# Attention block on one core: the causal mask of the diagonal score blocks moves from TensorE to ScalarE and GpSimd, and PSUM banks are handed over two at a time

## The reference

```
h = _layernorm(x, axis=-1) * (1 + ca) + sa
# inside the attention: q, k rotated, 16 heads of 8 channels
scores = jnp.einsum('bhqd,bhkd->bhqk', q, k) * scale
scores = jnp.where(causal_mask, -jnp.inf, scores)
attn = jax.nn.softmax(scores, axis=-1)
out = jnp.einsum('bhqk,bhkd->bhqd', attn, v)
...
x = x + ga * _L0_attn_ref(h, ...)
h = _layernorm(x, axis=-1) * (1 + cb) + sb
x = x + gb * _L0_ffn_ref(h, ...)
```

## Time and profile before

| | |
|---|---|
| median of 3 runs | 369.53 us (368.46 to 371.78) |
| span of the profiled execution, first to last instruction | 368.0 us (the page gives no other time of it) |
| busy in the span | PE 340.0, DVE 258.0, ACT 208.2, POOL 103.8 us |
| mean granted PE clock | 0.986 |

### The profile page before, as it was taken

The page is one execution under the profiler, slowest core; times in us unless marked ns, Lnnn a source line. Parts: engine busy times, 40 slices in busy tenths (PEclk is TensorE's granted clock), DMA queues, the critical chain, the costliest instruction groups (busy, mean ns, idle before and its releaser), DMA issues.

```text
span 368.0 us, 6868 instructions
## 1 busy us (share of the span) xinstructions
PE 340.0 (92%) x2332; PEld 160.5 (44%) x2360; DVE 258.0 (70%) x563; ACT 208.2 (57%) x399; POOL 103.8 (28%) x189
## 2 busy tenths in 40 slices
PE   6999789999799898999999989999999999899886
PEld 4545345443354432443543434344434445434555
DVE  4947667987999977587667878677887777423254
ACT  5350056754166666677356665864666665785341
POOL 3543253427410424401301212101204232443221
PEclk9999889999999999999899999999999999999999
DMA  6547512221410003340230500500000000000000
GB/s 202 184 118 189 139 44 69 67 67 25 113 44 0 3 1 73 74 101 0 67 89 6 130 2 2 131 1 30 1 2 3 3 3 1 4 0 3 28 2 29
DMA packets 13314, 18.87 MB, mean 51 GB/s; under 512 B 4192, under 2 KB 9184, under 8 KB 13280
## 3 DMA queue, kind: packets, MB, share of 16 engines
q1 hardware_dynamic: 12992, 18.04, 18.4%
q10 hardware_dynamic: 288, 0.39, 0.3%
HBM read 12.98 MB, written 5.24 MB: 50 GB/s over the span
## 4 chain that ended last, share of the span: by engine, by line
PE 67%; issue 9%; DVE 8%; POOL 3%; ACT 2%; DMA 0%; SPq 0%; ACTq 0%; POOLq 0%; DVEq 0%
PE ps_o L1066 18%; PE ps L1029 15%; PE ps L1046 13%; PE ps L1000 4%; PE ps L987 4%; DVE tmax L864 3%; PE ps L936 3%; PE ps L1024 2%; DVE rot L760 1%; PE ps L1008 1%; PE ps L993 1%; PE ps L927 1%; PE ps L940 1%; ACT pt L660 1%; PE ps L947 1%
## 5 line engine op out<-in xcount | busy, mean ns | idle before, releaser
L864 DVE TENSOR_REDUCE tmax<-ps 128x1 f32<-128x512 f32 (+3 forms) x304 | 186.4, 656 | 65.4 <-PE ps L1029 65.0
L660 ACT ACTIVATE pt<-ps 128x512 f32<-128x512 f32 (+1 forms) x304 | 161.9, 576 | 105.6 <-PE ps L1046 104.1
L1029 PE MATMUL ps<-kst,qst 72*128 72x128 bf16 (+3 forms) x576 | 113.9, 274 | 3.6 <-issue 2.2
L1046 PE MATMUL ps<-qst,kst 75*128 75x512 bf16 (+3 forms) x384 | 111.0, 327 | 4.9 <-DVE rot L760 1.8
L1066 PE MATMUL ps_o<-pt,v_sb 128*32 128x512 f32 (+3 forms) x768 | 83.5, 507 | 2.0 <-ACT pt L660 1.1
L1029 PEld LDWEIGHTS ps<-kst,qst 72*128 72x128 bf16 x576 | 49.1, 98 | 70.0 <-ACT pt L660 17.9
L556 POOL TENSOR_SCALAR_AFFINE_SELECT pt<-pt 128x512 f32<-128x512 f32 x64 | 40.4, 641 | 68.0 <-ACT pt L660 67.5
L1046 PEld LDWEIGHTS ps<-qst,kst 75*128 75x128 bf16 x384 | 34.9, 98 | 29.6 <-issue 6.4
L1008 PE MATMUL ps<-maska,identb 128*128 128x512 bf16 x118 | 34.1, 396 | 3.5 <-POOL maska L483 3.3
L521 POOL CAST negp<-negm 128x16 bf16<-128x16 f32 x16 | 3.2, 198 | 94.4 <-DVE negm L781 94.2
L1066 PEld LDWEIGHTS ps_o<-pt,v_sb 128*32 128x32 f32 x768 | 15.5, 108 | 32.2 <-issue 17.3
(11 more groups left out here) (102 smaller groups left out, 250.8 us busy)
## 6 DMA issues: line engine op xcount, KB each, us to landing
qst<-qparts SPq DMA_DIRECT2D x48, 96.0 KB
kst<-kparts SPq DMA_DIRECT2D x48, 96.0 KB
qparts<-part SPq DMA_DIRECT2D x16, 96.0 KB, 1.9
kparts<-part SPq DMA_DIRECT2D x16, 96.0 KB, 1.9
xs<-in_x SPq DMA_DIRECT2D x4, 256.0 KB, 7.2
rope_sb<-in_rope SPq DMA_DIRECT2D x2, 512.0 KB, 6.2
qparts<-part SPq DMA_DIRECT2D x16, 64.0 KB, 1.8
qst<-negt SPq DMA_DIRECT2D x48, 4.0 KB, 1.7
```

The costliest lines, as they stand in the source:

```text
L660: act.activation(pt[:, G % NP, h0:h0 + nh, 0:w], src, ACT.Exp, scale=SCALE).then_inc(s_exp, 1)
L864: dve.tensor_reduce(dst, src, AX.X, ALU.max).then_inc(s_max, 1)
L1029: last = pe.matmul(dst[:, j * nk:(j + 1) * nk], qst[0:ROWS, half, h, r * P:r * P + P], kst[0:ROWS, kh, h, k0:k0 + nk], start=(kind != "dia ...
L1046: last = pe.matmul(dst[:, j * w:(j + 1) * w], kst[:, kh, h, kt * P:kt * P + P], qst[:, half, h, c0:HALF], start=True, stop=True)
```

## The change

Three things change. First, the product with `maska` is gone from pass A. A diagonal pair of banks is copied by ACT from PSUM into a buffer `dg` in SBUF (`copy_diagonal`), masked there by POOL (`mask_diagonal`), and reduced by DVE from SBUF `DIAG_LAG` = 6 slots later. `dg` has two halves of 128x1024 and lies over buffers of the first stage (`pro`), so the first copy also waits for the gates. Second, banks go in units of two, in both passes: PE signals after the second bank of a unit, and DVE or ACT reads both with one instruction if they are neighbours in the ring (where the ring ends between them, with two). The two diagonal units of a step come first in its pass A. A unit is written in its first slot; the numbers of slots stay as they were. Third, PE takes pass B before pass A in a slot.

```
-def bank_jobs_a(half):
+def bank_units_a(half):
+    units = [("diag", [(r, 0), (r + 1, 0)], HG, P) for r in range(0, TU, 2)]
     for r in range(TU):
-        jobs.append(("diag", r, 0, HG, P))
         if r:
             nh = min(HG, HALF // (r * P)) if r < 3 else 1
-            jobs += [("tri", r, h, nh, r * P) for h in range(0, HG, nh)]
+            banks = [(r, h) for h in range(0, HG, nh)]
+            units += [("tri", banks[j:j + 2], nh, r * P) for j in range(0, len(banks), 2)]
         if half:
-            jobs += [("sq", r, h, 1, HALF) for h in range(HG)]
-    return jobs
+            units += [("sq", [(r, h), (r, h + 1)], 1, HALF) for h in range(0, HG, 2)]
+    return units
...
+UNIT_B = 2
+NB = 7
+DIAG_LAG = 6
...
-            for bank in grp[3]:
-                b_at[slot] = (s, gi, grp, bank, bank is grp[3][-1])
-                slot += 1
+            for j in range(0, len(grp[3]), UNIT_B):
+                unit = grp[3][j:j + UNIT_B]
+                b_at[slot] = (s, gi, grp, unit, unit[-1] is grp[3][-1])
+                slot += len(unit)
...
+    def operations(kind, i, n):
+        at = [use_no[(kind, (i, j))] % NB for j in range(n)]
+        return [(0, n)] if at == list(range(at[0], at[0] + n)) else [(j, 1) for j in range(n)]
...
+            def mask_diagonal(i):
+                n = diag_no[i]
+                pool.wait_ge(s_dcopy, diag_copies[i][-1])
+                d = dg[:, n % 2]
+                pool.affine_select(out=d, in_=d, compare_op=ALU.is_ge, fill=LOW, base=0,
+                                   pattern=[[0, 2 * HG], [-1, P]], channel_multiplier=1).then_inc(s_dmask, 1)
...
                 if i in b_at and b_at[i][4]:
                     zero_future(*b_at[i][0:3])
+                if i in diag_no:
+                    mask_diagonal(i)
...
+            def copy_diagonal(i):
+                n = diag_no[i]
+                act.wait_ge(s_a, unit_a[i] + 1)
+                if n == 0:
+                    act.wait_ge(s_gated, 1)
+                if n >= 2:
+                    act.wait_ge(s_dmax, n - 1)
+                for j, m in operations("a", i, 2):
+                    b0 = use_no[("a", (i, j))] % NB
+                    act.activation(dg[:, n % 2, HG * j:HG * (j + m)], ps[:, b0:b0 + m, :].rearrange("p b (h k) -> p (b h) k", k=P),
+                                   ACT.Copy).then_inc(s_dcopy, 1)
...
+                if i - DIAG_LAG in diag_no:
+                    s, (_, banks, _, _) = a_at[i - DIAG_LAG]
+                    n, r = diag_no[i - DIAG_LAG], banks[0][0]
+                    dve.wait_ge(s_dmask, n + 1)
+                    dve.tensor_reduce(tmax[STEPS[s][1]][:, s % 2, 0, r:r + 2],
+                                      dg[:, n % 2].rearrange("p (r h) k -> p r h k", h=HG), AX.X, ALU.max).then_inc(s_dmax, 1)
...
-                dst = take("a", i)
-                if kind == "diag":
-                    pe.matmul(dst, identb[:, :], maska[:, :, :].rearrange("p h k -> p (h k)"), start=True, stop=False,
-                              skip_group_check=True)
...
+                for n, (r, h0) in enumerate(banks):
+                    dst = take("a", (i, n))
...
-                if i in a_at:
-                    pass_a(i)
                 if i in b_at:
                     pass_b(i)
+                if i in a_at:
+                    pass_a(i)
```

More of the change, by code:

```diff
@@ L122, in plan @@
     for s, (b, half, g) in enumerate(STEPS):
-        for job in bank_jobs_a(half):
-            a_at[n] = (s, job)
-            n += 1
+        for unit in bank_units_a(half):
+            a_at[n] = (s, unit)
+            n += len(unit[1])
         a_end.append(n)
@@ L202, in adaln_block @@
         group_no.setdefault(b_at[i][0:2], len(group_no))
-    bank_no = {i: n for n, i in enumerate(sorted(b_at))}
+    unit_a = {i: n for n, i in enumerate(sorted(a_at))}
+    unit_b = {i: n for n, i in enumerate(sorted(b_at))}
+    b_slots = {i + j for i in b_at for j in range(len(b_at[i][3]))}
     prep_no = {u: n for n, u in enumerate(PREPS)}
@@ L209, in adaln_block @@
     for i in range(slots):
-        uses += [("a", i)] if i in a_at else []
-        uses += [("b", i)] if i in b_at else []
+        uses += [("b", (i, j)) for j in range(len(b_at[i][3]))] if i in b_at else []
+        uses += [("a", (i, j)) for j in range(len(a_at[i][1][1]))] if i in a_at else []
         uses += [("side", (st[0], st[1], k)) for st in pe_at.get(i, []) for k in range(BANKS_OF.get(st[0], 0))]
     use_no = {use: n for n, use in enumerate(uses)}
+    def operations(kind, i, n):
+        at = [use_no[(kind, (i, j))] % NB for j in range(n)]
+        return [(0, n)] if at == list(range(at[0], at[0] + n)) else [(j, 1) for j in range(n)]
+    diag_no = {i: n for n, i in enumerate(i for i in sorted(a_at) if a_at[i][1][0] == "diag")}
+    max_ops, exp_ops, n_max, n_exp = {}, {}, {}, {}
+    for kind, at, ops, after in (("a", a_at, max_ops, n_max), ("b", b_at, exp_ops, n_exp)):
+        total = 0
+        for i in sorted(at):
+            if i in diag_no and kind == "a":
+                continue
+            ops[i] = operations(kind, i, len(at[i][1][1] if kind == "a" else at[i][3]))
+            for j, n in ops[i]:
+                total += 1
+                for k in range(j, j + n):
+                    after[(i, k)] = total
+    diag_copies, total = {}, 0
+    for i in sorted(diag_no):
+        diag_copies[i] = []
+        for j, n in operations("a", i, 2):
+            total += 1
+            diag_copies[i] += [total] * n
+    max_end = {a_at[i][0]: n_max[(i, len(a_at[i][1][1]) - 1)] for i in sorted(a_at) if i not in diag_no}
+    exp_end = {b_at[i][0:2]: n_exp[(i, len(b_at[i][3]) - 1)] for i in sorted(b_at)}
     qparts = nc.dram_tensor("qparts", (B * 2, NG, 5, HD, HG, HALF), BF16)
@@ L666, in _ @@
                     exp(i)
+                if i in diag_no:
+                    copy_diagonal(i)
                 for st in stages.get(i, []):
@@ L1026, in pass_a @@
-                for j in range(nh):
-                    h = HG * g + h0 + j
-                    k0, kh = (r * P, half) if kind == "diag" else (0, half) if kind == "tri" else (0, 0)
-                    last = pe.matmul(dst[:, j * nk:(j + 1) * nk], qst[0:ROWS, half, h, r * P:r * P + P],
-                                     kst[0:ROWS, kh, h, k0:k0 + nk], start=(kind != "diag"), stop=True,
-                                     skip_group_check=True)
+                for n, (r, h0) in enumerate(banks):
+                    dst = take("a", (i, n))
+                    for j in range(nh):
+                        h = HG * g + h0 + j
+                        k0, kh = (r * P, half) if kind == "diag" else (0, half) if kind == "tri" else (0, 0)
+                        last = pe.matmul(dst[:, j * nk:(j + 1) * nk], qst[0:ROWS, half, h, r * P:r * P + P],
+                                         kst[0:ROWS, kh, h, k0:k0 + nk], start=True, stop=True)
@@ L1042, in pass_b @@
                     pe.wait_ge(s_mstack[s % 2], 48 * (s // 2 + 1))
-                dst = take("b", i)
-                for j in range(nh):
-                    h = HG * g + h0 + j
-                    last = pe.matmul(dst[:, j * w:(j + 1) * w], kst[:, kh, h, kt * P:kt * P + P],
-                                     qst[:, half, h, c0:HALF], start=True, stop=True)
+                for n, (h0, nh) in enumerate(unit):
+                    dst = take("b", (i, n))
+                    for j in range(nh):
+                        h = HG * g + h0 + j
+                        last = pe.matmul(dst[:, j * w:(j + 1) * w], kst[:, kh, h, kt * P:kt * P + P],
+                                         qst[:, half, h, c0:HALF], start=True, stop=True)
@@ L1078, in _ @@
             for i in range(slots):
+                if i in b_at:
+                    pass_b(i)
                 if i in a_at:
                     pass_a(i)
-                if i in b_at:
-                    pass_b(i)
-                if i not in b_at and i < max(a_at):
+                if i not in b_slots and i < a_end[-1] - 1:
                     keep_warm(1)
```

75 lines of the change are left out of this document (44 added, 31 removed).

## The result

The changed kernel takes 402.18 us (median of 4 runs, 398.98 to 405.01) against 370.65 for the kernel before, ratio 1.084 [1.079, 1.089]. The prediction was 379 us, range 363 to 392. Runs of one kernel differ in granted clock and so in time, by up to 4.7%; ratios leave out those over 1.5% above the kernel's fastest, medians do not, and the profiled executions of e1, e2, e4, e6, e7, e13 and e15 are such long ones.

A forecast was written before the change was run, and what follows sets the result against it. PE was taken to bound the kernel (340.0 of 368.0 us busy), with DVE close. Terms -7.0 - 3 + 4.8 + 5.2 + 7.6 + 2 = +9.6 on 368.0 gave 377.6, as a median 379 us; range 363 to 392.

The forecast's parts named there:

- The new waits are under 1 us each, and I count no lower clock for them: PE's added waits across the kernel: each under 1 us, with nothing added for a lower clock.
- the nothing (end: 3.5 us) for (0, 0): Four steps of (0, 0): removing 16 mask products counted as no gain, with 3.5 us as the other end.
- The margin in the ring: PSUM bank ring: paired reads free banks late, PE waits 0.32 us per clean pattern; +4.8 us together, bounds 2.4 to 7.5.
- 16 times with a side step ... which give the reader time: Ring patterns with side steps or narrower banks: 0 to 0.32 us of waiting each, taken as 0.15, 2.4 us together.
- POOL's order: Eight steps with `zero_future` ahead of POOL's four maxima operations: PE waits 0.65 us each, +5.2 us, bounds 0 and 8.
- The diagonal's place: Around the diagonal slots DVE idles, then runs late; PE waits 1.45 us at most of seven places, +7.6 us, bounds 0 and 11.
- the mask: Pass A on PE: dropping 32 mask products in half 1 saves 7.0 us; all 64 at most 14.1 us.
- ACT's copies at nothing: ACT's 32 diagonal copies, at most 1.20 us each, counted as hidden in idle time; up to 13 us if not.
- The short steps: Four steps of (1, 0): DVE needs 9.4 us against 8.72; 0.5 us more each, +2 us, bounds -3.5 and +5.
- The reads in pairs: DVE and ACT reading two banks at once: DVE pair 1.21 us, exponential pair 1.09; -3 us, other end -15.
- The forecast's sign and its reason: Whole kernel: slower, chance 0.60, as the margin, POOL's order and the diagonal's place cost more than the mask did.

The follow-up runs named there:

- e1: Kernel before without the mask product of the diagonal banks, maxima running over future keys too; ratio 0.990 to the kernel before.
- e2: Changed kernel with the mask product back on PE and diagonal banks read by DVE from PSUM, units of two kept; ratio 1.081 to the kernel before.
- e4: Changed kernel with three products without a reader in each of the first 46 slots; ratio 1.089 to the kernel before.
- e6: Changed kernel with the mask product on PE, pass A in units of one bank, pass B in units of two; ratio 1.031 to the kernel before.
- e7: Changed kernel with the mask product on PE, pass A in units of two banks, pass B in units of one; median 397.92 us, no ratio.
- e13: From the fifth step on, diagonal path alone, other units one bank; first four as before except pass B ahead of pass A everywhere; ratio 1.030 to the kernel before.
- e15: Change in the first four steps alone, later steps as before except pass B ahead of pass A in a slot; 388.56 us, ratio 1.048 to the kernel before.
- e5: Changed kernel with two products without a reader in each of slots 11 to 33; 394.38 us, ratio 1.066 to the kernel before.
- e17: Change in the first four steps alone, pass B first everywhere, one product without a reader in each of slots 11 to 33; 380.54 us, ratio 1.027 to the kernel before.
- e14: From the fifth step on, units of two with mask product on PE; first four as before except pass B ahead of pass A everywhere; ratio 1.056 to the kernel before.
- e8: Changed kernel with the mask product on PE and units of one bank in both passes, leaving only the new order; 376.74 us, ratio 1.017 to the kernel before.
- e18: Change in the first four steps alone, pass B first everywhere, two products without a reader in each of slots 11 to 33; 383.86 us, ratio 1.037 to the kernel before.
- e10: Changed kernel with POOL's zeroing of the future weights queued at the unit's last slot again; ratio 1.100 to the kernel before.
- e11: Change from the fifth step on; first four steps as before except pass B ahead of pass A in a slot; 389.31 us, ratio 1.055 to the kernel before.
- e3: Changed kernel with units of one bank in both passes, except diagonal pairs, still copied by ACT and masked by POOL; ratio 1.047 to the kernel before.
- e12: Kernel before without the 19 products without a reader of the first steps; ratio 1.003 to the kernel before.

## Why the prediction was wrong, step by step

**The step that failed first** is "The new waits are under 1 us each, and I count no lower clock for them", with the nothing (end: 3.5 us) for (0, 0). The waits for DVE are about as long as I said (6.0 us in 13, 1.1 at most), but stage B already had a window at 0.84, and what was priced was each wait, not what PE's clock does after several of them. The sum had nothing for B, +7.6 (-7.0 - 3 + 4.8 + 5.2 + 7.6) nearly all in C, and +2 for D. Measured: +14.7, +13.5 and +4.0. In B, some 12 us are the clock: B falls by 12.5 when fillers hold it up in the whole change (e5), and by about as much in the change of the first four steps (e17). The Trainium skill, TensorE: Matmul & The Clock Gate, A second HAM failure mode: psum-queue depth-cycling, tells of a kernel whose PE idles briefly between groups as it cycles through PSUM banks, and whose clock goes to and fro; the falls at 47.6 and 57.8, after 2.14 us of 3.50 and 1.74 of 3.40 with PE busy, agree; the 41 us at half speed that followed are no to and fro.

**The margin in the ring** was right as a mechanism and in its clean place (3.24 us, forecast about 3.2). In the sum, the waits for DVE's maxima were not the large ones: in C they come to 3.7 us in nine places, of each of which the overlap of PE's rows hides up to 0.16, where ring and diagonal had 12.4 (4.8 + 7.6). Yet the units of two, with the order, cost 15.7 us in C (e14), of which 10.2 us at half speed, against 3.4 before, explain at most 3.4. What I had backwards are the "16 times with a side step ... which give the reader time": there the pair delays DVE's work for the side step, and PE's waits for such work in C grow from 2.0 to 6.3 us (3.8 with the order alone, e8). **The order in a slot**, pass B ahead of pass A, had no term of its own: 3 to 5 us in C (e8 +4.6, e18 +5.0; up to 1.7 of each is clock).

**POOL's order**, +5.2, is refuted: 0 (e10). In C, PE waits 1.8 us in four places for POOL's chain, and waited 1.9 in three before.

**The diagonal's place and the mask.** DVE's pattern came as drawn. On top of the units, the diagonal path with the mask product gone gives C 12.1 - 15.7 = -3.6 us (e11, e14; up to 1.7 of it is 3.4 us less at half speed), where my terms made +0.6 (7.6 - 7.0). Without the units it gives C +4.0 (e3), where the order alone gives +4.6 (e8). So in C the path costs about nothing, and what e13 shows is mostly order and clock. With the order counted once (5.0, e18), and half of the half speed that e13 (20.5 us in C) and e14 (10.2) have over e11 (6.8) taken off, 9.0 + 15.7 - 5.0 - 6.8 - 1.7 = 11.2, an estimate, against 12.1 in e11. The mask product alone, at -7.0 for half 1, gave -2.9 in C, seven of its eight steps (e1, with 3.4 us at half speed there as before). **ACT's copies at nothing**: their cover is thin. PE waits 5.6 us in five places for the maxima's rows, but e14, without copies, waits 5.9 in six, so it is not the copies alone that make these rows late.

**The short steps**: +2 forecast (bounds -3.5 and 5), +4.0 measured, +3.4 without the 2.9 us at half speed (e5); e13 gives 3.5 and e14 1.8 of it.

**The reads in pairs** had the right prices: 1.21 us forecast for a pair and for a masked read, 1.219 and 1.208 measured; an exponential of a pair 1.09, measured 1.024. Groups by form after:

```profile
L710 ACT ACTIVATE pt<-ps 128x1024 f32<-128x1024 f32 x99 | 101.0, 1024 | 93.6 <-PE ps L1123 93.4
L940 DVE TENSOR_REDUCE tmax<-ps 128x2 f32<-128x1024 f32 x55 | 66.6, 1219 | 33.6 <-PE ps L1106 33.4
...
L927 DVE TENSOR_REDUCE tmax<-pro 128x8 f32<-128x1024 f32 x32 | 38.7, 1208 | 0.0
```

DVE got 8.9 us back (258.0 to 249.1) and the steps got longer, so the -3 found no place. The forecast's sign and its reason, readers that finish later in a ring of seven, held; the delay of side work, the order in a slot and the late rows of the maxima had no term, and the clock lay outside all bounds. **Open** remain the clock's exact share (the fillers cost time too), which part lets it fall (in B it is at half speed for 10.2 us in e8, 13.7 in e3, 27.3 in e1, 34.1 in e2 and 47.8 after the change, so several parts do, and none of them as much as the whole), what makes the maxima's rows late, and why pass A's pairs seem to weigh more than pass B's.

## What to carry to other kernels

Where PE's granted clock is already below 1.00 in a stage, price a change there by what PE has to do in it, not by each wait; giving PE more to do shortened the run here (e5, e17). Larger reads save the reader's time, but everything behind them in the engine's queue comes later too: look for side work that frees a bank. When fillers are tried against a low clock, try two doses, since too many look like no effect. When a change is taken apart, ask what every part still holds: here the new order stood in all of them, and the parts seemed not to add.

## What the hardware showed that was not expected

The clock did not come back when PE's rows were continuous: in the changed kernel it stayed at 0.50 from 57.8 to 98.8 us, with PE shown busy for all of 62.43 to 98.80, while in the kernel before it fell for 3.4 us at a time and in e12 for 10.2 and 6.8, and rose again. In stage B of the change in the first four steps alone, what stood between 41.0 us at half speed (e15) and none (e17) was 15 short products.
